# Cross-attention: scores with the keys on partitions, and an output projection one and a half bodies later

## The reference

```python
a = _layer_norm(audio_kv, ln_gamma, ln_beta)
Q = (hidden_states @ Wq.T).reshape(B, Tt, HEADS, HEAD_DIM).transpose(0, 2, 1, 3)
K = (a @ Wk.T).reshape(B, Ta, HEADS, HEAD_DIM).transpose(0, 2, 1, 3)
V = (a @ Wv.T).reshape(B, Ta, HEADS, HEAD_DIM).transpose(0, 2, 1, 3)
scores = jnp.einsum('bhtd,bhsd->bhts', Q, K) * scale
scores = jnp.where(mask, scores, jnp.float32(-jnp.inf))
attn = jax.nn.softmax(scores, axis=-1)
out = jnp.einsum('bhts,bhsd->bhtd', attn, V)
out = out.transpose(0, 2, 1, 3).reshape(B, Tt, D)
return hidden_states + jnp.tanh(gate) * (out @ Wo.T)
```

## Time and profile before

| | |
|---|---|
| time, median of 3 runs | 2214.16 us (2211.24 to 2214.3) |
| profiled execution, and its span | 2215.14 us, 2213.3 us |
| mean granted clock of PE | 0.998 |
| PE matmul busy | 2172.1 us, 98% |
| DVE busy | 1556.1 us, 70% |
| ACT busy | 1170.6 us, 53% |
| POOL busy | 561.4 us, 25% |
| matmuls | 10752, of them 2560 transposes |

### The profile page before, as it was taken

One profiled execution on the slowest core, in us unless ns is written; L12 is line 12 of the kernel. 1 busy time (PEld: TensorE's weight loads), 2 busy tenths in 40 slices (PEclk: granted clock), 3 DMA queues, 4 the chain that ended last, 5 costly groups with the idle time before them and its releaser, 6 DMA issues.

```text
span 2213.3 us, 36066 instructions
## 1 busy us (share of the span) xinstructions
PE 2172.1 (98%) x10752; PEld 1789.4 (81%) x10752; DVE 1556.1 (70%) x3040; ACT 1170.6 (53%) x2338; POOL 561.4 (25%) x661
## 2 busy tenths in 40 slices
PE   5999999999999999999999999999999999999998
PEld 4888878888888888888888888888888888888886
DVE  5666786667766677666776668666687666866666
ACT  4655664545645456445554456454474544744544
POOL 5444531113311133111231013211141110511111
PEclk9999999999999999999999999999999999999999
DMA  6567555553544635555355544545445454354441
GB/s 248 180 229 269 196 167 175 172 190 124 177 154 162 199 115 181 172 159 173 131 179 175 164 163 138 172 161 190 152 142 172 163 188 152 122 191 133 142 152 67
DMA packets 111803, 370.02 MB, mean 167 GB/s; under 512 B 14624, under 2 KB 15648, under 8 KB 110880
## 3 DMA queue, kind: packets, MB, share of 16 engines
q1 hardware_dynamic: 111776, 369.69, 50.3%
HBM read 285.75 MB, written 50.33 MB: 152 GB/s over the span
## 4 chain that ended last, share of the span: by engine, by line
PE 93%; DVE 3%; ACT 1%; issue 1%; DMA 1%; SPq 0%; POOL 0%; DVEq 0%
PE pj L455 15%; PE pj L459 15%; PE pj L457 15%; PE so L374 11%; PE pt L391 9%; PE pv L401 5%; PE pv L402 5%; PE so L423 3%; PE so L418 3%; PE so L419 3%; PE pv L418 3%; PE pv L419 3%; PE pv L423 3%; PE pj L382 1%; PE pt L473 1%
## 5 line engine op out<-in xcount | busy, mean ns | idle before, releaser
L841 POOL TENSOR_SCALAR prob<-prob,rinv 128x512 f32<-128x512 f32 x512 | 354.2, 707 | 1394.0 <-DVE rinv L686 1392.8
L706 DVE TENSOR_TENSOR pt_lo<-pt,pt_hi 128x512 fp32r<-128x512 f32 x512 | 353.7, 691 | 222.9 <-ACT pt_hi L569 216.7
L681 DVE CUSTOM_DVE_ANT_0 prob<-so,mask_add 128x512 f32<-128x512 f32 x512 | 351.2, 691 | 196.7 <-PE so L374 186.9
L548 ACT ACTIVATE prob<-prob,nmax 128x512 f32<-128x512 f32 x512 | 369.8, 723 | 170.3 <-DVE nmax L681 165.9
L569 ACT CAST pt_hi<-pt 128x512 fp32r<-128x512 f32 x512 | 300.6, 587 | 243.1 <-PE pt L391 242.6
L455 PE MATMUL pj<-a_hi,w_hi 128*128 128x512 f32 x1024 | 416.9, 407 | 3.6 <-POOL a_lo L868 2.2
L457 PE MATMUL pj<-a_lo,w_hi 128*128 128x512 f32 x1024 | 416.6, 407 | 0.0
L459 PE MATMUL pj<-a_hi,w_lo 128*128 128x512 f32 x1024 | 411.5, 402 | 0.0
L374 PE MATMUL so<-k_st,q_st 128*128 128x512 f32 x1024 | 323.8, 398 | 5.1 <-DMA k_st<-k_st 4.2
L391 PEld LDWEIGHTS pt<-ident,prob 128*128 128x128 f32 x2048 | 254.4, 140 | 70.5 <-POOL prob L841 1.3
L391 PE MATMUL pt<-ident,prob 128*128 128x128 f32 x2048 | 306.3, 272 | 0.9 <-POOL prob L841 0.9
(11 more groups left out here) (74 smaller groups left out, 3043.5 us busy)
## 6 DMA issues: line engine op xcount, KB each, us to landing
w_hi<-kept_hi SPq DMA_DIRECT2D x224, 512.0 KB, 3.7
w_lo<-kept_lo SPq DMA_DIRECT2D x224, 512.0 KB, 5.4
k_st<-k_st SPq DMA_DIRECT2D x256, 128.0 KB, 4.0
cx<-in_ctx SPq DMA_DIRECT2D x32, 512.0 KB, 5.4
xy<-in_xT SPq DMA_DIRECT2D x32, 512.0 KB, 4.9
kept_hi<-w_hi SPq DMA_DIRECT2D x32, 512.0 KB, 5.6
kept_lo<-w_lo SPq DMA_DIRECT2D x32, 512.0 KB, 6.8
out_y<-xy SPq DMA_DIRECT2D x7, 2048.0 KB, 11.8
```

The source lines that it names most:

```text
L548: act.activation(prob[:, u], prob[:, u], ACT.Exp, bias=nmax[:, u:u + 1], scale=-1.0, accum_out=rsum[:, u:u + 1]).then_inc(exp_done, 1)
L681: dve.tensor_tensor_reduce(prob[:, u], so[u % 2][:], mask_add[:], -SCALE, BIG, ALU.add, ALU.min, nmax[:, u:u + 1]).then_inc(so_read, 1)
L706: dve.tensor_tensor(pt_lo[:, u % 2], pt[u % 2][:], f32(pt_hi[:, u % 2]), ALU.subtract).then_inc(pl_done, 1)
L841: pool.tensor_scalar(prob[:, u], prob[:, u], rinv[:, u:u + 1], 1.0, ALU.mult, ALU.mult).then_inc(scale_done, 1)
```

## The change

The scores are computed with a block of 128 *keys* on the partitions and the 512 queries along the row, so that the exponentials are already as the product with V wants them. `turn_p` is gone. The maximum and the sum over the keys now run across partitions:

- `block_maxima`: a reduction with a transpose of 32 x 32 squares in its input, over two blocks (1024 columns of PSUM) at a time; `key_maxima` joins the four blocks. PE turns the small result (`maxima_turned`), `group_maxima` takes two more maxima, PE turns it back (`maxima_back`), `spread_maxima` spreads it over the partitions, and `subtract` takes it from the scores, 1024 columns at a time.
- the sums: POOL adds the four blocks (`key_sums`), DVE reduces with a transpose (`column_sums`), SP sends the result to HBM and back in one and four small transfers (`exchange_sums`), DVE sums, inverts and spreads them (`inverse_sums`), and POOL scales the values' result (`o_scale`) in place of the probabilities.
- `p_low` moves from DVE to POOL; `exp`, `p_high` and `accumulate` take two blocks in one instruction.
- a body has two halves, one for each head `h`. The product with V of a head stands in the next half (`values(*before, ...)`), and the output projection of pair k begins in the second half of body k + 1 and ends in the first of body k + 2 (`out_step`), into the banks `sc` that the scores use too. After the last body a `drain` does what is left.
- `swap_k` and its transfers go; `q_high` and `k_high` write each part twice instead.

```diff
-FILL_S = (0, 4, 4, 4, 4, 4, 5, 5)
-FILL_T = (4, 2, 2, 2, 2, 2, 2, 2)
-FILL_GAP = (4, 12)
-FILL_O = (1, 1, 1, 1, 1, 1, 2, 0)
...
+FILL = ((2, 2, 4, 4, 2, 22), (2, 2, 8, 2, 2, 20))
...
+            def exchange_sums(k):
...
+                sp.wait_ge(rq_done, k * 2 + 2)
...
+                sp.dma_start(sums.rearrange("p h b -> p (h b)"), rq[:].rearrange("p h b -> p (h b)")).then_inc(rd_done, 16)
+                sp.wait_ge(rd_done, k * 16 + 16)
...
+                for g in range(4):
+                    sp.dma_start(r_four[32 * g:32 * (g + 1)],
+                                 sums[:, g // 2].rearrange("(c j) b -> j c b", c=4)).then_inc(rx_done, 16)
...
+            def scores(k, h, kind):
+                if h == 0:
...
+                ge(pe, acc_done, k * 4 - (4 if h else 6))
+                for i in range(2):
+                    ge(pe, sub_done, k * 4 + 2 * h + i - 1)
...
+                        pe.matmul(sc[:, s], kt[:, h, 0, cols], qt[:, h, 0], start=True, stop=False)
+                        mm = pe.matmul(sc[:, s], kt[:, h, 1, cols], qt[:, h, 1], start=False, stop=True)
+                    mm.then_inc(s_done, 1)
...
+            def maxima_turned(k, h):
+                pe.wait_ge(mc_done, k * 2 + h + 1)
+                ge(pe, oadd_done, k * 2 + h - 1)
+                pe.transpose(pv[h][:, 0, 0:P], m_cols[:], ident[:]).then_inc(mf_done, 1)
...
+            def maxima_back(k, h):
+                pe.wait_ge(mr_done, k * 2 + h + 1)
+                pe.transpose(pv[h][:, 0, P:2 * P], m_rows[:].rearrange("p c i -> p (c i)"), ident[:]).then_inc(mt_done, 1)
...
-            def turn_p(k, u, kind):
...
-                pe.wait_ge(pl_done, k * UNITS + (u + 1))
-                for t in range(TB):
-                    mm = pe.transpose(pt[u % 2][:, t * P:(t + 1) * P], prob[:, h * TB + t, s * P:(s + 1) * P],
-                                      ident[:])
...
+            def values(k, h, i):
...
+                pe.wait_ge(pl_done, k * 4 + 2 * h + i + 1)
...
+                    pe.matmul(pv[h][:, 0], w, p_hi[:, s], start=s == 0, stop=False)
+                    mm = pe.matmul(pv[h][:, 0], w, p_lo[:, s], start=False, stop=s == TB - 1)
+                mm.then_inc(pv_done, 1)
...
+                    if n == 0 and c == 0:
+                        pe.wait_ge(ol_done, q + 1)
+                    mm = pe.matmul(dst, w_hi[:, slot, cols], o_lo[:], start=False, stop=True)
+                mm.then_inc(op_done, 1)
...
+            def out_step(k, h, p, kind):
...
+                    pe.wait_ge(sub_done, k * 4 + 2 * h + p + 1)
...
+                if h and p == 0:
+                    pe.wait_ge(oh_done, k)
...
+                    f = FILL[h]
...
+                    scores(k, h, kind)
+                    take(stream, f[0])
+                    before = (k, 0) if h else (k - 1, 1)
+                    started = h or not (isinstance(k, int) and k == 0)
+                    if started:
+                        values(*before, 0)
+                    maxima_turned(k, h)
+                    take(stream, f[1])
+                    maxima_back(k, h)
+                    take(stream, f[2])
+                    if started:
+                        values(*before, 1)
+                    if h == 0:
...
-                for u in range(UNITS):
-                    turn_p(k, u, kind)
-                    take(stream, FILL_T[u])
-                    if u:
-                        values(k, u - 1)
...
+                    take(stream, f[3])
+                    out_step(k, h, 0, kind)
...
+                    take(stream, f[4] if kind != "prepare" else f[4] + 4)
+                    out_step(k, h, 1, kind)
...
+                    take(stream, f[5] if kind != "prepare" else f[5] - 4)
...
+            def exp(k, h, i):
+                act.wait_ge(sub_done, k * 4 + 2 * h + i + 1)
+                p = prob[:, h, 2 * i:2 * i + 2]
+                act.activation(p, p, ACT.Exp, scale=SCALE).then_inc(exp_done, 1)
+
+            def p_high(k, h, i):
+                act.wait_ge(exp_done, k * 4 + 2 * h + i + 1)
+                ge(act, pv_done, k * 4 + 2 * h + i - 1)
+                act.copy(p_hi[:, 2 * i:2 * i + 2], prob[:, h, 2 * i:2 * i + 2]).then_inc(ph_done, 1)
...
+                ge(act, s_done, k * 4 + 2 * h + 2)
+                half, other = halves[h], halves[1 - h]
+                act.copy(qt[half, h, 0], pj[1][half, 0]).then_inc(qh_done, 1)
+                act.copy(qt[other, h, 0], pj[1][half, 0]).then_inc(qh_done, 1)
...
-                act.copy(o_tmp[dst], pv[h][src]).then_inc(otmp_done, 1)
+                act.wait_ge(pv_done, k * 4 + 2 * h + 2)
...
-                act.copy(o_hi[:], o32[:]).then_inc(oh_done, 1)
+                act.wait_ge(om_done, k + 1)
...
+                o_move(k, 0)
+                exp(k, 1, 0)
+                if not last:
                     k_high(k, 0)
+                p_high(k, 1, 0)
+                exp(k, 1, 1)
+                if not last:
                     k_high(k, 1)
...
-            def row_max(k, u):
...
-                dve.tensor_tensor_reduce(prob[:, u], so[u % 2][:], mask_add[:], -SCALE, BIG, ALU.add, ALU.min,
-                                         nmax[:, u:u + 1]).then_inc(so_read, 1)
...
+            def block_maxima(k, h, i):
+                dve.wait_ge(s_done, k * 4 + 2 * h + i + 1)
+                dve.tensor_reduce(out=mq[:, 2 * i:2 * i + 2], in_=sc[:, 2 * i:2 * i + 2].rearrange(
+                    "p s (b j) -> p s b j", j=32), op=ALU.max, axis=mybir.AxisListType.X,
+                    apply_transpose=True).then_inc(mq_done, 1)
...
+            def key_maxima(k, h):
+                dve.wait_ge(mq_done, k * 4 + 2 * h + 2)
+                dve.tensor_reduce(out=m_cols[:, 0:16], in_=mq[:].rearrange("p s b -> p b s"), op=ALU.max,
+                                  axis=mybir.AxisListType.X).then_inc(mc_done, 1)
...
+            def group_maxima(k, h):
+                dve.wait_ge(mf_done, k * 2 + h + 1)
+                dve.tensor_reduce(out=m_two[0:16], in_=pv[h][0:16, 0, 0:P].rearrange("p (a i) -> p i a", a=2),
+                                  op=ALU.max, axis=mybir.AxisListType.X).then_inc(mg_done, 1)
...
+            def spread_maxima(k, h):
+                dve.wait_ge(mt_done, k * 2 + h + 1)
+                dve.transpose(m_b[:].rearrange("p (b i) -> p b i", i=32),
...
+            def subtract(k, h, i):
+                dve.wait_ge(mb_done, k * 2 + h + 1)
+                dve.tensor_tensor(prob[:, h, 2 * i:2 * i + 2], sc[:, 2 * i:2 * i + 2],
+                                  m_b[:].rearrange("p (o t) -> p o t", o=1).to_broadcast((P, 2, T)),
...
+            def column_sums(k, h):
+                dve.wait_ge(sum_done, k * 4 + 2 * h + 2)
+                dve.tensor_reduce(out=rq[:, h], in_=prob[:, h, 0].rearrange("p (b j) -> p b j", j=32), op=ALU.add,
+                                  axis=mybir.AxisListType.X, apply_transpose=True).then_inc(rq_done, 1)
...
+            def inverse_sums(k):
+                dve.wait_ge(rx_done, k * 64 + 64)
+                dve.tensor_reduce(out=r_sum[:], in_=r_four[:].rearrange("p c b -> p b c"), op=ALU.add,
...
+                dve.transpose(r_b[:].rearrange("p (b i) -> p b i", i=32),
+                              r_inv[:].rearrange("p (b o) -> p b o", o=1).to_broadcast((P, 16, 32))).then_inc(rb_done, 1)
...
+                block_maxima(k, 0, 0)
+                block_maxima(k, 0, 1)
+                key_maxima(k, 0)
+                if begun:
+                    column_sums(k - 1, 1)
+                group_maxima(k, 0)
+                spread_maxima(k, 0)
+                subtract(k, 0, 0)
+                subtract(k, 0, 1)
+                v_low(k)
+                if begun:
+                    o_add(k - 1, 1)
+                accumulate_both(k, b, j, 0, kind)
...
                 if not last:
                     q_low(k, 0)
...
+                if begun:
+                    inverse_sums(k - 1)
+                block_maxima(k, 1, 0)
+                block_maxima(k, 1, 1)
+                key_maxima(k, 1)
+                if not last:
+                    q_low(k, 1)
+                group_maxima(k, 1)
+                spread_maxima(k, 1)
+                subtract(k, 1, 0)
+                subtract(k, 1, 1)
+                o_add(k, 0)
+                accumulate_both(k, b, j, 1, kind)
+                if not last:
                     k_low(k, 0)
...
+            def p_low(k, h, i):
...
+                pool.tensor_tensor(p_lo[:, 2 * i:2 * i + 2], prob[:, h, 2 * i:2 * i + 2], f32(p_hi[:, 2 * i:2 * i + 2]),
+                                   ALU.subtract).then_inc(pl_done, 1)
+
+            def key_sums(k, h):
+                pool.tensor_tensor(prob[:, h, 0:2], prob[:, h, 0:2], prob[:, h, 2:4], ALU.add).then_inc(sum_done, 1)
+                pool.wait_ge(sum_done, k * 4 + 2 * h + 1)
+                pool.tensor_tensor(prob[:, h, 0], prob[:, h, 0], prob[:, h, 1], ALU.add).then_inc(sum_done, 1)
...
```

(59 more changed lines are left out.)

867 lines of the change are left out of this document (413 added, 454 removed).

## The result

The changed kernel takes 2554.47 us (median of 4 runs, 2552.14 to 2557.08) against 2214.23 (4 runs, 2211.24 to 2216.12): ratio 1.154, 95% interval 1.152 to 1.156. The forecast was 2,420, its range 2,240 to 2,570. The first rows are of the page of the kernel after, and answer to the earlier trace rows.

What follows compares the result with a forecast made beforehand. PE's pace bounds the kernel before; after, a four-engine chain of 34.7 us a plain body. 46 + 249 + 1,492 + 570 + 6 + 57 = 2,420 us, 9% slower, range 2,240 to 2,570.

Steps and rivals of the forecast that it cites:

- a dearer transposing maximum: Rival, chance 0.18: a transposing maximum takes 2.3 us, not 1.22; body 36.9, total 2,560 to 2,590.
- the clock: Rival, chance 0.10: PE's clock falls once a body behind the wait of 2.3 us, adding 88 us: 2,510.
- six bodies of the first batch: Plain bodies with weight splits on ACT and POOL, two in one chain: 41.5 us each, 249 in all.
- seven prepare and seven switch: Bodies around the change of batch: prepare 41.4 us, switch 40.0, 570 for seven pairs, plus 6 for splits in the first.
- last body and drain: After the last sums, 35.5 us into the last body: exchange, inverse, scaling, 24 matmuls, accumulate and store; 57 us.
- The period: Time from one plain body to the next: 34.7 us, not PE's own 30.3, with four PE waits and restarts of 4.4.
- both links: Chain steps in a plain body: ACT's o_move(k, 0) ahead of exp(k, 1, 0), and column_sums ahead of the next group_maxima.
- the walk: Step-by-step sum of the plain body's chain through PE, DVE, ACT and POOL, from the second half's first score: 34.7 us.
- What I add to the others: Work added to other engines, per body: DVE 25 us, POOL from 5.4 to 19.7, ACT near 16; none full at 30.3.
- The exchange: exchange_sums' transfers through HBM: 6.5 to 11 us, hidden by some 11.6; at 13 they would cost 0.8.
- Faster: Rival, chance 0.14: key_sums ends before key_maxima and the maximum's steps are cheaper; 30.6 us a body, 2,160 in all.
- PE waits only where it must: Condition of the faster rival: in plain bodies only the waits of 0.7 and 0.5 us a half remain.

Runs made afterwards that it cites:

- e2: Changed kernel with exp(k, 1, 0) placed ahead of o_move(k, 0) on ACT: 2489.1 us, plain bodies 33.8 to 34.0 but one.
- e1: Changed kernel with column_sums(k-1, 1) moved on DVE from ahead of the first half's group_maxima to behind its two subtractions: 2499.2 us.
- e7: Changed kernel with sums later, exponential first, m_rows (L677) from one input, and PE's projections dealt out otherwise (FILL): 2335.6 us, plain bodies 30.9 to 31.0.
- e9_all: Changed kernel with e7's edits, mask_rows earlier, batch loop written out, context loaded one body earlier, work moved to POOL's and DVE's free times: 2180.8 us.
- e6: Changed kernel with the loop over batches 1 to 6 written out six times on every engine: 2528.4 us.
- e3: Changed kernel with L677, which writes m_rows, reading one tensor in place of two: 2506.2 us, plain bodies 34.1.
- e8: Kernel before, with three of the four transposes of every turn_p left out (result not the reference's): 2119.4 us, 31.57 a body.
- e10: e9_all with POOL's four x_low behind its p_low, and nmean and vpe on POOL: 2170.4 us, ratio 0.980 to the kernel before.

## Why the prediction was right, and where it was not

The time lies in the range, near its slow edge. The part of the range above 2,475 was there for a dearer transposing maximum and for the clock; the first did not come (L663 takes 1.23), the second came in part, and most of the 134 us of error came from a term that no rival doubted. That it still fell inside is in part luck. The span by the prediction's own terms; the terms in between are measured between `turn_v`s, 1.5 us more than between scores:

| term | predicted | measured |
|---|---|---|
| start, to the first scores | 46 | 46.5 |
| six bodies of the first batch | 249 | 253.5 |
| 43 plain bodies | 1,492 | 1,524 |
| seven prepare and seven switch | 576 | 673 |
| last body and drain | 57 | 54.6 |

- **The direction and its cause** were right: PE has less to do and waits for a chain through all four engines. Its prices held: L663 1.23 (said 1.22), L689 1.22, L734 1.28, L695 0.71, L901 2.40, L907 1.32 (1.26 at the least), ACT's exponential 1.06 and cast 1.05.

```profile
L663 DVE TRANSPOSE_TENSOR_REDUCE mq<-sc 128x32 f32<-128x1024 f32 x256 | 305.6, 1230 | 140.1 <-PE sc L346 122.0
...
L689 DVE TENSOR_TENSOR prob<-sc,m_b 128x1024 f32<-128x1024 f32 x256 | 301.5, 1219 | 4.4
```

- **The period** of 34.7 was met, and both links put to the test moved it the way the walk says: e2 by what it says to 0.1 us, e1 by two thirds of it. Details differ: PE's wait in `maxima_back` was 1.57, not 2.3, and the other 1.17, not 0.5, since L677, priced 0.25, took 0.28 in the first half and 0.90 in the second, where POOL was at work. The two errors cancelled. Two more did: PE's waits make 3.8 us in place of 4.2, and its own work is not 30.3 but 31.0, as e7 shows. The 34.7 is the right chain, but its last tenths are luck.
- **"What I add to the others"**, at the change of batch, is the step that was mis-sized: 576 against 673. (The 39.2 and 34.7 read in the earlier trace rows are the first batch's; in the others the kernel before takes 37.8 and 33.6, once 34.5.) DVE's low parts had been priced at the 0.69 of L706, which reads one of its inputs from PSUM, in a kernel where POOL worked for a quarter of the time; there DVE's `a_low` and `x_low` took 0.79 and 0.75. Now `a_low` took 2.1, `x_low` 1.77, the two mask rows 4.8 in place of "two instructions, 1.6", `nmean` 2.0 (in e9_all). The added work of POOL, 5.4 to 19 us a body, is what made them meet. The prediction counted POOL's time as free since POOL was not full. In the switch interval at 663.8 PE waits 4.4 us for `a_lo` and 4.4 for the mask rows. The Trainium skill, SBUF — State Buffer, section "Who interferes with whom", has the rule that it should have weighed: a DVE instruction with two SBUF inputs contends with a POOL instruction that reads SBUF, and a copy, cast or `tensor_scalar` in a two-port mode contends with POOL too; whoever issues first holds the shared ports for the whole instruction. The traces agree (0.27 against up to 1.93 for L677; 0.77 against 1.86 for `x_low`; `q_low` and `k_low`, with one input in PSUM, take 0.68 beside POOL and 0.69 apart from it).
- **The jump** at the end of the batch loop, 3.4 us of DVE's issue five times, was in no term (e6: 26 us with what followed). The kernel before has loops too, but there PE waits for DVE only 9.0 us in all.
- **The clock**, a rival at 0.10, came in part: plain bodies average 35.45, of which the six with statistics make 0.4 and the rest, some 17 us in all, are bodies of 35.8 to 36.3. The window from 475 to 511 has one, its granted clock 0.96, and matmuls that follow each other by 0.43 us (1.2 GHz) behind a wait of 1.57. The body at 545.5 waited as long, at 1.00. What decides it the runs do not show. In e2, e3 and e7, where PE waits for the maxima in a body 3.0, 3.2 and 0 us in all against 3.8, the plain bodies of the later batches show no such drop (but for one in e2); in e1, where it waits 2.7, seven of them do, as the one at 836, with a granted clock of 0.95 and eight matmuls 0.43 apart behind a wait of 1.16. The clock has a part in the mis-sized term as well: it is 0.90 and 0.88 in the prepare and switch windows above, and in the latter 20 matmuls follow each other by 0.43 in place of 0.23, up to 4 us of an interval that is 10 too long. How much of that the waits behind them hide is open.
- **The exchange** was hidden, as said: `r_four` landed 1.7 us after issue and was waited for once, 1.4 us, 16 us before the end.
- **"Faster", 0.14**, and "PE waits only where it must": 30.6 a body was said for it, and e7 reached 31.0. It needed four edits for that, and more at the change of batch, to get under 2,214.

Left open: what the last of the clock's drops cost and what brings them about; how the first batch's remaining prepare interval of 44.7 to 48.2 us divides between splits and waits, and whether other placements of `a_low` would bring the last 6 us a batch.

## What to carry to other kernels

When work moves to an engine with spare time, price it together with what runs beside it: in these runs DVE and POOL had spare time only one after the other where a DVE instruction read two SBUF tensors, or was a copy or a `tensor_scalar` within SBUF. Read one operand from PSUM, use a reduction, or put such an instruction where POOL waits for somebody. Find the link that closes a chain across the loop's edge; moving that one instruction (`column_sums`, 1.1 us a body) and giving PE matmuls between two turns (1.8) was worth more than leaving out three quarters of the transposes (1.7, e8). And look at the rare bodies first: 14 of 64 carried three quarters of the error.

## What the runs showed of the hardware

- A 16x128 `tensor_tensor` on DVE of 0.28 us takes up to 1.93 beside POOL; a `tensor_scalar` of four columns, 0.17 at the start, takes up to 2.02 (in e9_all). Both end with POOL's instruction.
- POOL pays too: two `x_low` took 1.72 each beside DVE's (e9_all), 1.30 in e10, where DVE's stood elsewhere.
- A reduction with transpose runs at the pace of a plain one: 1.23 us for 1,024 columns of PSUM, and 0.71 for 512 of SBUF, where the plain one of `mask_factor` takes 0.69. It does not slow beside POOL: L663 takes 1.21 to 1.25 in the 193 places where POOL works all the while, and in the 37 where it does not work at all.
- At the end of the batch loop, with its long body, DVE stands 3.36 to 3.47 us in issue, five times; with the loop written out (e6) not once.
